# The output copies of unit 0 between the first and the second Gelu on ScalarE

## The chip, the core and the metric

One core of a Trainium2 chip (trn2) runs the whole program in one launch. The metric is the device time of one execution in microseconds. The median of three runs is 2313.62 us (2309.42 to 2320.92).

## The reference

The input x is (16, 128, 128) in float32: 16 batches of 128 tokens with 128 features. Four blocks follow one another, each added to x: a cross attention with 16 heads, a network of six layers, a second cross attention with a gate, and a network of two layers. The change lies in the six-layer network. Each of its layers is a local attention with 16 heads and then a feed-forward part:

```python
for i in range(DEPTH):                       # 6
    x = attn_layer(shift_tokens(x), Wqkv[i], q_scale[i], k_scale[i], Wo[i]) + x
    x = ffn_layer(shift_tokens(x), ln_g[i], ln_b[i], W1[i], b1[i], W2[i], b2[i]) + x
...
def ffn_layer(x, g, bln, W1, b1, W2, b2):
    ...
    hg = xn @ W1 + b1
    a, gate = jnp.split(hg, 2, -1)
    return a * jax.nn.gelu(gate, approximate=False) @ W2 + b2
```

Attention normalises q and k, rotates them, masks scores to windows of 32 tokens, takes a softmax and multiplies by v. The hidden width of the feed-forward part is 341, so a gate has 341 columns.

## The kernel before

Everything stays on chip; each engine has a queue written out by hand, in program order, and semaphores order the queues among each other. The first network runs as a software pipeline over 96 units: 6 layers times 16 batches. A unit's 16 heads are two halves of 8, which the code calls i = 0 and i = 1. In step s, `step_0(s)` of each engine handles the projections and the rotation of unit s, the transposes and (for i = 0) the scores of unit s - 1, and the rest of the attention of units s - 2 and s - 3.

For i = 0 the chain is as follows. TensorE computes the scores of unit s - 1 (`scores_all`, L751 and L757) at the end of step s. In step s + 1, which treats it as unit s - 2, ScalarE takes the Exps (`exponents_all`, L1475, first in its step), VectorE the reciprocal of the sums (L2051), GpSimd the division, TensorE the transposes (L766) and then the values (`values_all`, L780, the last work of its step). ScalarE copies the result from banks 7 and 6 of PSUM with `outputs(0, s - 2)`, two ACTIVATEs of L1506, 128x256 each. Its wait is for `AT["o"][0]`, raised by the last matmul of the values.

In the next step TensorE runs keys and queries (L700, two each at this data type: four matmuls), and then projects the values of the next unit into bank 7 (L700 as well). Bank 7 must have been copied, so that projection waits for `AT["oe"][0]`, which the second copy raises. Then follow the transposed probabilities of i = 1 (L766), a piece of the feed-forward part, a transpose of queries (L721), and the scores of i = 1, which wait for both Exp groups of i = 0 (`AG["ex"][0][0]` and `[1]`), because those read banks 3 and 4.

The feed-forward part works on groups of 4 batches, 24 groups in the first network, each spread over 4 steps; `ff_phase` gives c, the step within the group. With c == 2 the gate's three chunks (128, 128 and 85 columns) are projected (L850), VectorE copies them out (L2102), and ScalarE evaluates three Gelus in place (`ff_gelu`, L1531), each behind its own `FF["ge"]`. With c == 3 comes the up projection (L860), and VectorE multiplies it with the Gelus (L2108), chunk by chunk, each behind its `FF["gelu"]`. The step c == 2 occurs 23 times in `step_0` (s = 9, 13, ..., 97); the 24th group's Gelus are in `between`.

The end of ScalarE's step before the change:

```python
if live(s - 1):
    turned(1, s - 1, 1)
    turned(1, s - 1, 0)
if c == 2 and f >= 0:
    ff_gelu(f)
if live(s - 2):
    outputs(0, s - 2)
```

Of the kernel before, what the change touches and what calls it, by code (L numbers as in the profile page):

```python
# [8 lines left out]
ACT = mybir.ActivationFunctionType  # L9
# [14 lines left out]
CH = [(0, 128), (128, 128), (256, HID - 256)]  # L24
# [6 lines left out]
LAST = 4 * NLAYER - 1  # L31
GATE, UP = (3, 4, 5), (6, 7, 2)
# [33 lines left out]
def build(nc, A, out):  # L66
# [9 lines left out]
    with ExitStack() as ctx:  # L76
        sb = lambda name, shape, dt=F32: ctx.enter_context(nc.sbuf_tensor(name, shape, dt))
        sem = lambda name: ctx.enter_context(nc.semaphore(name))
        bank = [ctx.enter_context(nc.psum_tensor(f"bank{i}", [P, BLK], F32)) for i in range(8)]
# [15 lines left out]
        b1 = [sb(f"b1_{i}", [P, 6]) for i in range(2)]  # L95
# [49 lines left out]
        gl = [slot(39 + c) for c in range(3)]  # L145
# [29 lines left out]
        FF = {n: sem("ff_" + n) for n in "x mean cen sq var rstd bc xn aff up ge gelu hid y z outer".split()}  # L175
# [26 lines left out]
        def nth(i, p):  # L202

            return p + 1 if i == 0 else p + 1 - PHASES[1]["lo"]
# [9 lines left out]
        def at(eng, sem_, n):  # L214

            if n > 0:
                eng.wait_ge(sem_, n)

        def ff_phase(ph, s):

            t = s - ph["lo"]
            first, steps, groups = (7, 4, 24) if ph["net"] == 0 else (5, 2, 8)
            if t < first:
                return -1, -1, -1
            g, c = divmod(t - first, steps)
            f = 4 * ph["layer0"] + g
            return c, f if g < groups else -1, f - 1 if 1 <= g <= groups else -1
# [1120 lines left out]
        def _(act):  # L1348
# [89 lines left out]
            def act_phase(ph):  # L1438
# [28 lines left out]
                def exponents_all(i, p):  # L1467

                    at(act, AG["pt"][i][0], p - 1)
                    at(act, AG["ri"][i][0], p - 1)  # L1470
                    for g in range(2):
                        act.wait_ge(AG["mx"][i][g], p + 1)
                        for j in range(4):
                            h = 2 * j + g
                            ins = nc.scalar.activation(pb[i][0][p % 2][:, h * DH:(h + 1) * DH], bank[3 + g][:, j * DH:(j + 1) * DH],  # L1475
                                                       ACT.Exp, bias=amx[p % 2][:, i, h:h + 1], accum_out=asum[p % 2][:, i, h:h + 1])
                        ins.then_inc(AG["ex"][i][g], 1)
# [19 lines left out]
                def outputs(i, p):  # L1497

                    act.wait_ge(AT["o"][i], p + 1)
                    if ni == 0:  # L1500
                        at(act, AT["y"][0], p)
                    else:
                        at(act, AT["y"][i], nth(i, p - 1))
                    if ni == 0:
                        for half in range(2):
                            ins = nc.scalar.activation(o_t[i][:, 256 * half:256 * half + 256], bank[7 - half][:, 0:256], ACT.Copy)  # L1506
                        ins.then_inc(AT["oe"][i], 1)
                    else:
                        nc.scalar.activation(o_t[i], bank[7][:], ACT.Copy).then_inc(AT["oe"][i], 1)
# [11 lines left out]
                    nc.scalar.activation(fxn, fxn, ACT.Identity, scale=lnp[w][:, 0:1], bias=lnp[w][:, 1:2]  # L1521
                                         ).then_inc(FF["aff"], 1)

                def ff_gelu(f):
                    for c in range(3):
                        w = CH[c][1]
                        if f < LAST:
                            act.wait_ge(FF["ge"], 3 * f + c + 1)
                        else:
                            act.wait_ge(FF["up"], 6 * f + c + 1)  # L1530
                        nc.scalar.activation(gl[c][0:w, :], gl[c][0:w, :] if f < LAST else bank[GATE[c]][0:w, :], ACT.Gelu, bias=b1[f // 4 % 2][0:w, 3 + c:4 + c]  # L1531
                                             ).then_inc(FF["gelu"], 1)

                def step_0(s):
                    c, f, before = ff_phase(ph, s)
                    if live(s - 2):
                        exponents_all(0, s - 2)
                        values(0, s - 2)
                    if live(s - 3):
                        probs_all(1, s - 3)  # L1540
                    if live(s):
                        square(0, s, 1)
                        square(0, s, 0)
                    if s == 0:
                        gate_weights()
                    if live(s - 1):
                        turned(0, s - 1, 0)
                    if live(s - 3):
                        outputs(1, s - 3)
                    if s in (1, 3, 5):  # L1550
                        g_square(act, (s + 1) // 2, (s + 1) // 2)
                    if c == 0 and f >= 0:
                        ff_square(f)
                    if c == 1 and f >= 0:
                        ff_affine(f)
                    if live(s - 2):
                        exponents_all(1, s - 2)
                    if live(s):
                        square(1, s, 1)
                        square(1, s, 0)  # L1560
                    if live(s - 1):
                        turned(0, s - 1, 1)
                    if s == hi:
                        for k in range(2):
                            g_square(act, 4 + k, k)
                    if live(s - 2):
                        probs_all(0, s - 2)
                        values(1, s - 2)
                    if live(s - 1):
                        turned(1, s - 1, 1)  # L1570
                        turned(1, s - 1, 0)
                    if c == 2 and f >= 0:
                        ff_gelu(f)
                    if live(s - 2):
                        outputs(0, s - 2)

                def step_1(s):
                    c, f, before = ff_phase(ph, s)
                    if live(s - 3):
                        outputs(1, s - 3)  # L1580
                    if live(s - 2):
                        exponents(1, s - 2, 0)
                        probs(0, s - 2, 0)
                        exponents(1, s - 2, 1)
                    if live(s):
                        square(0, s, 0)
                    if live(s - 1):
                        turned(0, s - 1, 0)
                        turned(0, s - 1, 1)
                    if s - lo in (1, 3):  # L1590
                        n = 10 + (s - lo - 1) // 2
                        g_square(act, n, n - 8)
                    if c == 0 and f >= 0:
                        ff_square(f)
                    if live(s):
                        square(0, s, 1)
                    if live(s - 2):
                        values(0, s - 2)
                        probs(0, s - 2, 1)
                    if c == 1 and f >= 0:  # L1600
                        ff_gelu(f)
                    if live(s - 1):
                        exponents(0, s - 1, 1)
                        exponents(0, s - 1, 0)
                    if live(s - 2):
                        probs(1, s - 2, 1)
                        probs(1, s - 2, 0)
                    if live(s):
                        square(1, s, 0)
                    if c == 0 and f >= 0:  # L1610
                        ff_affine(f)
                    if live(s - 2):
                        values(1, s - 2)
                    if live(s - 1):
                        turned(1, s - 1, 1)
                    if live(s):
                        square(1, s, 1)
# [4 lines that stand above are left out]
# [48 lines left out]

            t0, ff0_square, ff0_affine, ff0_gelu = act_phase(PHASES[0])
            t1, _a, _b, _c = act_phase(PHASES[1])

            def between(s, part):

                if (s, part) == (1, 1):
                    ff0_square(23)
                if (s, part) == (2, 1):
                    ff0_affine(23)
                    g_square(act, 6, 2)  # L1680
                if (s, part) == (3, 2):
                    ff0_gelu(23)
                if (s, part) == (5, 1):
                    g_square(act, 7, 3)
                if s in (7, 9) and part == 0:
                    n = 8 + (s - 7) // 2
                    g_square(act, n, n - 8)
# [764 lines left out]
```

## Time and profile before

| | us |
|---|---|
| median of 3 runs | 2313.62 |
| lowest and highest run | 2309.42, 2320.92 |
| the profiled execution | 2317.28 |
| its span, first to last instruction | 2315.5 |

| engine | busy, share of the span |
|---|---|
| TensorE, matmuls (PE) | 2135.8 us, 92% |
| TensorE, weight loads (PEld, beside PE) | 1456.9 us, 63% |
| VectorE (DVE) | 1759.7 us, 76% |
| ScalarE (ACT) | 1708.7 us, 74% |
| GpSimd (POOL) | 1339.4 us, 58% |

One execution was recorded. A row of a timeline gives the start in us from the start of the span, the duration, the engine, the line of the program, the operation, the tiles written and read, and in brackets the idle time of the engine before it with what ended it. "issue" means that the engine waited for nothing that the profile shows. Matmul rows of one line that follow each other are merged (xN), and so are activations; instructions of one engine overlap a little, so N of them take less than N durations. Shares of busy time are averages over stages with different limits, so the waits and one place in order of time say more than the table.

### The profile page before, as it was taken

Reading aid. Unit: us, or ns where it says so; the run is one execution under the profiler, and the core shown is the slowest. Engines: PE = TensorE matmul, PEld = TensorE weight load, DVE = VectorE, ACT = ScalarE, POOL = GpSimd, SP = SyncE. Lnnn points to the kernel's source line nnn. Section 1 sums busy time; section 2 is a strip of 40 time slices with the busy share of each in tenths; the row PEclk is TensorE's granted clock in tenths of the full one; section 3 lists DMA queues with packets and bytes.
Section 4 is the critical chain, followed back from the end, with each engine's and each line's share of the span. In section 5 each row is a group of like instructions: output and inputs, shape, how many; then the busy total and the mean of one; then the engine's idle time right before and its main releaser. Section 6 shows DMA issues by size and latency. Waiting matters only on the chain. (4 is left out here: it accounts for less than half of the span.)

```text
span 2315.5 us, 88378 instructions
## 1 busy us (share of the span) xinstructions
PE 2135.8 (92%) x33770; PEld 1456.9 (63%) x33770; DVE 1759.7 (76%) x4937; ACT 1708.7 (74%) x5910; POOL 1339.4 (58%) x1270
## 2 busy tenths in 40 slices
PE   7989999999999989999999999999999886899997
PEld 5656666666666666666666666666666664666663
DVE  4888777778777878777777777877777477887863
ACT  3757787877788877787787787877787544788783
POOL 1347666666666666666666666766666124666650
PEclk8999999999999999999999999999999998999999
DMA  4001221112211222112211122111221100000000
GB/s 111 4 3 40 67 57 46 39 47 66 56 41 40 64 50 55 40 43 62 55 48 43 44 66 58 47 38 43 53 52 41 44 13 7 13 13 15 15 11 23
DMA packets 144687, 96.93 MB, mean 42 GB/s; under 512 B 61928, under 2 KB 137232, under 8 KB 144272
## 3 DMA queue, kind: packets, MB, share of 16 engines
q1 hardware_dynamic: 143120, 91.02, 15.5%
q8 instruction: 274, 4.49, 0.8%
q14 instruction: 141, 1.16, 0.2%
q10 hardware_dynamic: 1152, 0.26, 0.1%
HBM read 23.11 MB, written 1.05 MB: 10 GB/s over the span
## 5 line engine op out<-in xcount | busy, mean ns | idle before, releaser
L700 PE MATMUL bank<-wqkv,hs 128*128 128x512 f32 x1344 | 675.1, 621 | 19.0 <-ACT arena L1506 13.5
L1779 POOL TENSOR_TENSOR arena<-arena,rnorm 128x512 f32<-128x512 f32 x448 | 455.2, 1044 | 388.7 <-DVE rnorm L2028 387.5
L1772 POOL TENSOR_TENSOR arena<-arena 128x512 f32<-128x512 f32 x448 | 567.0, 1273 | 140.4 <-DVE arena L1977 140.4
L1475 ACT ACTIVATE arena<-bank,amx 128x64 f32<-128x64 f32 x1536 | 457.5, 334 | 8.3 <-DVE amx L2043 8.0
L1972 DVE TENSOR_TENSOR arena<-bank,rot 128x512 f32<-128x512 f32 x448 | 306.7, 685 | 88.9 <-PE bank L700 85.3
L700 PEld LDWEIGHTS bank<-wqkv,hs 128*128 128x128 f32 x1344 | 230.9, 193 | 207.1 <-issue 158.1
L1452 ACT ACTIVATE arena<-bank 128x512 f32<-128x512 f32 x448 | 263.9, 616 | 131.3 <-PE bank L721 130.1
L1475 ACT ACTIVATION_READ_ACCUMULATOR arena<-bank,amx 128x1 f32 x1536 | 351.1, 229 | 0.0
L1977 DVE TENSOR_TENSOR arena<-bank,rot 128x256 f32<-128x256 f32 x896 | 333.4, 413 | 0.0
L721 PEld LDWEIGHTS bank<-ident,arena 128*128 128x128 f32 x1792 | 212.9, 142 | 151.7 <-issue 128.5
L1984 DVE TENSOR_REDUCE ss<-arena 128x8 f32<-128x512 f32 x448 | 283.3, 669 | 31.2 <-ACT arena L1446 31.0
L1446 ACT ACTIVATE arena<-bank 128x512 f32<-128x512 f32 x448 | 265.0, 644 | 44.5 <-DVE arena L1977 44.0
L1786 POOL TENSOR_TENSOR arena<-arena,ainv 128x512 f32<-128x512 f32 x192 | 200.3, 1043 | 165.4 <-DVE ainv L2051 165.4
L721 PE MATMUL bank<-ident,arena 128*128 128x128 f32 x1792 | 251.7, 275 | 12.5 <-POOL arena L1779 5.8
L1506 ACT ACTIVATE arena<-bank 128x256 f32<-128x256 f32 x384 | 127.1, 387 | 178.7 <-PE bank L780 177.8
L813 PEld LDWEIGHTS bank<-arena,wo 128*128 128x128 f32 x1792 | 220.9, 194 | 56.5 <-issue 50.0
L780 PE MATMUL bank<-arena 64*64 64x32 f32 (+1 forms) x9216 | 186.3, 221 | 51.3 <-issue 50.0
L813 PE MATMUL bank<-arena,wo 128*128 128x128 f32 x1792 | 225.7, 278 | 3.1 <-ACT arena L1506 2.6
L780 PEld LDWEIGHTS bank<-arena 64*64 64x64 f32 x9216 | 160.7, 134 | 73.2 <-issue 56.5
L2043 DVE TENSOR_REDUCE amx<-bank 128x4 f32<-128x256 f32 x384 | 143.8, 416 | 39.7 <-PE bank L757 39.4
L757 PE MATMUL bank<-arena 64*32 64x64 f32 (+1 forms) x12288 | 168.7, 217 | 0.0
L757 PEld LDWEIGHTS bank<-arena 64*32 64x32 f32 x12288 | 154.8, 105 | 0.3
(179 smaller groups left out, 3224.5 us busy)
## 6 DMA issues: line engine op xcount, KB each, us to landing
arena<-arena SPq DMA_DIRECT2D x768, 64.0 KB
wqkv<-in_L_ffn_Wqkv_dram SPq DMA_DIRECT2D x24, 256.0 KB, 3.1
hs<-z SPq DMA_DIRECT2D x128, 32.0 KB, 1.8
fx<-z SPq DMA_DIRECT2D x32, 128.0 KB, 2.2
hs<-z SPq DMA_DIRECT2D x128, 31.8 KB, 1.9
fx<-z SPq DMA_DIRECT2D x32, 127.0 KB, 2.5
wqkv<-in_L_ffn_Wqkv_dram SPq DMA_DIRECT2D x24, 128.0 KB, 2.5
w<-in_L_ffn_W_dram SPq DMA_DIRECT2D x6, 341.0 KB
```

Source lines behind the costliest of these rows:

```text
L700: nc.tensor.matmul(bank[o][:], src[:], wqkv[w][:, off:off + 512], start=True, stop=True).then_inc(AT[name] if part < 2 else AT[name][i], 1)
L721: mm = nc.tensor.transpose(bank4[o][:, j, :], rc[i][c][p % 2][:, j * P:(j + 1) * P], ident[:])
L757: mm = nc.tensor.matmul(bank[3 + g][q:q + 32, DH * j:DH * j + n], q_t[i][rows, P * j + q:P * j + q + 32], k_t[i][rows, P * j + key:P * j + ...
L780: mm = nc.tensor.matmul(bank4[7 - half][to:to + DH, j, q0:q1], src[g][rows, DH * h:DH * h + DH], pbt[i][0][rows, h * P + q0:h * P + q1], s ...
L813: mm = nc.tensor.matmul(bank4[7][:, 0, :], wo[w][:, i, j, :] if ni == 0 else wo[w][:, j // 2, j % 2, :], o_t[i][:, j * P:(j + 1) * P], sta ...
L1446: nc.scalar.activation(sq[i][c], bank[c][:], ACT.Square).then_inc(AT["sqk" if c else "sqq"], 1)
L1475: ins = nc.scalar.activation(pb[i][0][p % 2][:, h * DH:(h + 1) * DH], bank[3 + g][:, j * DH:(j + 1) * DH], ACT.Exp, bias=amx[p % 2][:, i, ...
L1772: nc.gpsimd.tensor_tensor(t, t, rs[i][c], ALU.add).then_inc(AT["ak" if c else "aq"][i], 1)
L1779: nc.gpsimd.tensor_tensor(t, t, rnorm[p % 2][:, i, HU * c:HU * c + HU].unsqueeze(2).to_broadcast([P, HU, DH]), ALU.mult).then_inc(AT["mk" ...
L1972: nc.vector.tensor_tensor(heads(rc[i][c][p % 2]), src, r[:, 2 * c, :].unsqueeze(1).to_broadcast([P, HU, DH]), ALU.mult)
L1977: ins = nc.vector.tensor_tensor(dst, src[:, :, (1 - a) * hd:(2 - a) * hd], r[:, 2 * c + 1, a * hd:(a + 1) * hd].unsqueeze(1).to_broadcast( ...
L1984: nc.vector.tensor_reduce(ss[:, i, HU * c:HU * c + HU], heads(sq[i][c]), AX.X, ALU.add).then_inc(AT["ssk" if c else "ssq"], 1)
```

## The change

On ScalarE, `ff_gelu(f)` ran a loop over three chunks; `ff_gelu(f, c)` now runs one chunk. In `step_0`, `outputs(0, s - 2)` stood behind the three Gelus and now stands behind the first. In `step_1` (second network) and in `between` (the 24th group) the three calls are made in a loop, in the order of before. No other engine's program is changed.

```diff
--- before.py
+++ after.py
@@ -1521,15 +1521,15 @@
                     nc.scalar.activation(fxn, fxn, ACT.Identity, scale=lnp[w][:, 0:1], bias=lnp[w][:, 1:2]
                                          ).then_inc(FF["aff"], 1)
 
-                def ff_gelu(f):
-                    for c in range(3):
-                        w = CH[c][1]
-                        if f < LAST:
-                            act.wait_ge(FF["ge"], 3 * f + c + 1)
-                        else:
-                            act.wait_ge(FF["up"], 6 * f + c + 1)
-                        nc.scalar.activation(gl[c][0:w, :], gl[c][0:w, :] if f < LAST else bank[GATE[c]][0:w, :], ACT.Gelu, bias=b1[f // 4 % 2][0:w, 3 + c:4 + c]
-                                             ).then_inc(FF["gelu"], 1)
+                def ff_gelu(f, c):
+
+                    w = CH[c][1]
+                    if f < LAST:
+                        act.wait_ge(FF["ge"], 3 * f + c + 1)
+                    else:
+                        act.wait_ge(FF["up"], 6 * f + c + 1)
+                    nc.scalar.activation(gl[c][0:w, :], gl[c][0:w, :] if f < LAST else bank[GATE[c]][0:w, :], ACT.Gelu, bias=b1[f // 4 % 2][0:w, 3 + c:4 + c]
+                                         ).then_inc(FF["gelu"], 1)
 
                 def step_0(s):
                     c, f, before = ff_phase(ph, s)
@@ -1570,9 +1570,12 @@
                         turned(1, s - 1, 1)
                         turned(1, s - 1, 0)
                     if c == 2 and f >= 0:
-                        ff_gelu(f)
+                        ff_gelu(f, 0)
                     if live(s - 2):
                         outputs(0, s - 2)
+                    if c == 2 and f >= 0:
+                        ff_gelu(f, 1)
+                        ff_gelu(f, 2)
 
                 def step_1(s):
                     c, f, before = ff_phase(ph, s)
@@ -1598,7 +1601,8 @@
                         values(0, s - 2)
                         probs(0, s - 2, 1)
                     if c == 1 and f >= 0:
-                        ff_gelu(f)
+                        for chunk in range(3):
+                            ff_gelu(f, chunk)
                     if live(s - 1):
                         exponents(0, s - 1, 1)
                         exponents(0, s - 1, 0)
@@ -1679,7 +1683,8 @@
                     ff0_affine(23)
                     g_square(act, 6, 2)
                 if (s, part) == (3, 2):
-                    ff0_gelu(23)
+                    for c in range(3):
+                        ff0_gelu(23, c)
                 if (s, part) == (5, 1):
                     g_square(act, 7, 3)
                 if s in (7, 9) and part == 0:
```

## Rows read from the trace of the kernel before

**Rows 1.** The page: the span; busy time, share of it and instructions by engine.
```profile
span 2315.5 us, 88378 instructions
...
PE 2135.8 (92%) x33770; PEld 1456.9 (63%) x33770; DVE 1759.7 (76%) x4937; ACT 1708.7 (74%) x5910; POOL 1339.4 (58%) x1270
```

**Rows 2.** Groups of ScalarE: line, operation, shape, count | busy us, mean ns | idle before.
```profile
L1531 ACT ACTIVATE arena<-arena,b 128x512 f32<-128x512 f32 x62 | 41.3, 714 | 0.4
L1531 ACT ACT_TABLE_LOAD x31 | 39.8, 1283 | 0.5
...
L1475 ACT ACT_TABLE_LOAD x22 | 28.2, 1283 | 0.4
```

**Rows 3.** Waits of TensorE in the whole run: total us, times, longest.
```profile
PE bank L780 <- issue: 50.0, 66, 3.4
...
PE bank L700 <- ACT arena L1506: 13.5, 16, 0.9
```

**Rows 4.** ScalarE in time, one place: start, us, line, operation, [idle before].
```profile
506.45 0.66 ACT L1506 ACTIVATE arena<-bank 128x256 f32<-128x256 f32 x2 [1.75 <-PE bank L780]
...
513.23 1.08 ACT L1452 ACTIVATE arena<-bank 128x512 f32<-128x512 f32 x2
514.33 1.28 ACT L1531 ACT_TABLE_LOAD   x1
515.63 1.95 ACT L1531 ACTIVATE arena<-arena,b 128x512 f32<-128x512 f32 x3
517.48 0.63 ACT L1506 ACTIVATE arena<-bank 128x256 f32<-128x256 f32 x2
518.13 1.28 ACT L1475 ACT_TABLE_LOAD   x1
519.42 0.31 ACT L1475 ACTIVATE arena<-bank,amx 128x64 f32<-128x64 f32 x1
...
521.65 0.24 ACT L1475 ACTIVATION_READ_ACCUMULATOR arena<-bank,amx 128x1 f32 x1
```

**Rows 5.** TensorE in time, the same place.
```profile
505.99 0.42 PE L780 MATMUL bank<-arena 64*64 64x32 f32 x11 [0.71 <-issue]
...
514.49 0.90 PE L780 MATMUL bank<-arena 64*64 64x64 f32 x48
515.32 1.99 PE L700 MATMUL bank<-wqkv,hs 128*128 128x512 f32 x4
518.16 1.13 PE L700 MATMUL bank<-wqkv,hs 128*128 128x512 f32 x2 [0.85 <-ACT arena L1506]
...
521.99 0.30 PE L751 MATMUL bank<-mask_b,ident_b 64*32 64x256 bf16 x8 [0.97 <-issue]
```

**Rows 6.** VectorE in time, the same place.
```profile
521.98 0.20 DVE L2051 RECIPROCAL ainv<-asum 128x8 f32<-128x8 f32 x1 [2.39 <-issue]
522.10 0.74 DVE L2108 SCALAR_TENSOR_TENSOR arena<-bank,b,arena 128x512 f32<-128x512 f32 x1
...
528.62 0.75 DVE L2108 SCALAR_TENSOR_TENSOR arena<-bank,b,arena 128x512 f32<-128x512 f32 x1 [0.57 <-PE bank L860]
```

**Rows 7.** First, largest and last late place: the Gelus, then TensorE's values.
```profile
305.87 1.95 ACT L1531 ACTIVATE arena<-arena,b 128x512 f32<-128x512 f32 x3
...
306.27 0.67 PE L780 MATMUL bank<-arena 64*64 64x32 f32 x32 [1.16 <-issue]
...
1061.28 1.95 ACT L1531 ACTIVATE arena<-arena,b 128x512 f32<-128x512 f32 x3
...
1062.16 0.42 PE L780 MATMUL bank<-arena 64*64 64x32 f32 x11 [1.25 <-issue]
...
1753.45 1.95 ACT L1531 ACTIVATE arena<-arena,b 128x512 f32<-128x512 f32 x3
...
1753.96 0.66 PE L780 MATMUL bank<-arena 64*64 64x32 f32 x28 [1.11 <-issue]
```

## The prediction

> **What bounds the kernel now.** I read the page first. TensorE is busy 92% of the span and ScalarE 74% [rows 1], so a gain has to come out of TensorE's idle time, or out of a stretch where ScalarE sets the pace. The change touches 23 places, one step in four of the first network's 96 units: the step in which ScalarE evaluates the three Gelus of a feed-forward group. So the next view is what ScalarE spends on Gelus [rows 2], then the waits of the whole run [rows 3], then one such place in order of time on ScalarE [rows 4], TensorE [rows 5] and VectorE [rows 6], and last the places that look different [rows 7].
>
> TensorE waited 13.5 us in all, 16 times, for the output copies of L1506 before a projection of L700 [rows 3]. By the trace 15 of these waits lie right behind the Gelus, 0.82 to 0.87 us each; this is the wait that the edit can remove. In the place near 514 us, ScalarE turns queries (L1452), loads the Gelu table from 514.33, runs three Gelus from 515.63, makes the two output copies from 517.48, loads the Exp table from 518.13, and runs 8 Exps from 519.42; their last record ends at 521.65 + 0.24 = 521.89 [rows 4]. The reader is to see that no row from 513.23 to there has idle time before it: ScalarE runs 8.7 us without a pause. TensorE meanwhile ends its values at 514.49 + 0.90 = 515.39, ends the next step's four key and query matmuls at 517.31, waits 0.85 us for the copies until 518.16, and then waits again, 0.97 us, before the scores at 521.99 [rows 5]. That second wait ends 0.10 us behind the Exps; `scores_all` waits there for both groups of them, since they read the score banks that it overwrites. The profile calls it "issue", but the program's wait and the time agree. VectorE also stands still, 2.39 us, and resumes at 521.98 with the reciprocals of the Exps' sums [rows 6]. So here ScalarE's queue, from the Gelu table to the last Exp, is the path, and TensorE has 0.85 + 0.97 us of slack in it.
>
> **The change part by part.** It adds and removes no instruction and no wait. On ScalarE the two copies go ahead of the second and third Gelu, in the 23 steps with c == 2; the rewritten calls in `step_1` and `between` give the old order. TensorE's, VectorE's, GpSimd's and SyncE's queues are the same, and ScalarE issues no DMA here.
>
> The copies come earlier. A Gelu starts about (1.95 - 0.71) / 2 = 0.62 us behind the one before [rows 2, 4], so the copies can start 1.24 us sooner, at 516.25, and end at 516.9. TensorE is busy until 517.31, so its wait of 0.85 us goes. What is late next is the second wait: projection, transposes and the up projection all move 0.85 us forward, and then TensorE stands 0.97 + 0.85 = 1.82 us before the scores, for the last Exp is where it was. VectorE is held by the same Exps. Gain: 0.00 us per place. The rest of ScalarE's queue up to the last Exp holds the same work in another order, so its length is the same but for how neighbours overlap: the load would follow a Gelu (0.71 us long, 0.62 us apart) and no longer a copy. I take zero; the overlap of two neighbours is about 0.1 us by these rows, so the bounds are -0.1 and +0.1 us per place, -2.3 and +2.3 us in 23.
>
> The second and third Gelu come 0.65 us later. Their readers are the products with the up projection on VectorE (L2108). The first of these starts at 522.10 and needs only the first Gelu, which doesn't move; the second starts at 528.62, the third behind it [rows 6]. Cost nothing; were this cover gone, at most 0.65 us per place.
>
> The copies wait for TensorE's values (L780), and now the Gelus and Exps are queued behind that wait. In 15 places the values end about 0.86 us before the second Gelu's old start (515.39 against 516.25 [rows 4, 5]) and the wait is open. In 7 places TensorE stands for 0.83 to 1.25 us in the middle of the values, a stall that the profile calls "issue", and the values end later: at 306.27 + 0.67 = 306.94 in the first, where the second Gelu began at 305.87 + 0.62 = 306.49, so 0.44 us too late (unrounded starts); 0.67 us in the largest (1062.58 against 1061.90) and 0.54 in the last [rows 7]. The four others, read the same way, give 0.57, 0.28, 0.52 and 0.32. Sum 3.34 us. A waiting copy starts 0.04 us behind the values' end (506.45 against 505.99 + 0.42 [rows 4, 5]): 7 * 0.04 = 0.28. Before the change a Gelu filled this time; now ScalarE idles, and the Exps, TensorE's scores and VectorE's reciprocals come later by as much. In these places TensorE doesn't wait for the copies now, so nothing is given back. The cost may be less where a later stall of TensorE swallows it; such a stall, of 1.4 us or more, stands 2 to 3 us behind the Exps in two of the seven (the sizes 0.67 and 0.32), so the bounds are 2.5 and 3.6 us. I take 3.6, since TensorE's queue has no spare time between most of these scores and the next step. The 23rd place closes the phase, its values are ready in time and no scores stand behind it; I cost it at zero.
>
> Sum: 0 + 3.6 = +3.6 us. Against the profiled execution, 2317.28 us with a span of 2315.5 us, this is 2320.9. That execution is 3.7 us over the median of the runs, 2313.62 us; on the median the sum gives 2317.2 us.
>
> **The rivals.**
> A. TensorE's wait is worth its length. If the stretch were TensorE's and not ScalarE's, each of the 15 waits would come off the time: 13.5 * 15 / 16 = 12.7 us, less the 3.6 us that rival A would also deny (TensorE would have slack for them). Time 2300.9. For it speaks that TensorE is the busiest engine; against it the 0.97 us wait right behind, which ends with the Exps. It decides if the scores don't wait for Exps there. A half-way case, in which some of the 0.85 us survives because stalls of TensorE shift, gives about 2307.
> B. Slower: the stall inside the values meets more places. Stalls before L780 sum to 50.0 us in 66 waits [rows 3], and only 7 of 23 places have one now. It costs from the point where the values end behind the second Gelu's start, 0.86 us later than in an open place; the smallest stall among the seven, 0.83 us, already ends them 0.28 + 0.86 = 1.14 us later, so this point lies at a stall of some 0.55 us. If all 23 places had it, at the mean of the seven, (3.34 + 0.28) / 7 = 0.52 us, the cost would be 11.9 us, time 2325.5. Against it: TensorE's own stream is unchanged, and the work ahead of these values too.
> C. Slower: the copy between two Gelus forces the tables to change. A load is 1.28 us [rows 2]; two more per place, 23 * 2 * 1.28 = 59 us, time 2373. Against it: the copies already follow the third Gelu with no load between (517.48), and the load stands only before the first Exp [rows 4].
> The Trainium skill, in "ScalarE: Activation LUTs", section "Table sets: the hidden batching unit", tells authors to group activations by table set and finish one before switching, which speaks against putting another function between two Gelus; but it also lists copy among the cheap functions present in every set, and the trace agrees, with 0 loads between Gelu and copy. By the same page's section on the load, a switch costs about 2.66 us with its drain, which would make C some 122 us; the trace has 0.02 us between the turned keys' end and the load.
> D. The change doesn't do what it says. If the built queue kept the old order, the time would stay at 2313.6 us; against it, the queue in the trace follows the program's order call by call [rows 4].
>
> **How the numbers follow.** Forecast (0 to +6 us, nothing gained behind the copies) 0.80; A 0.07; half-way 0.03; B 0.06; C 0.02; D 0.02. Predicted: 2317.2. The likeliest case's own bounds are 2.5 - 2.3 = +0.2 and 3.6 + 2.3 = +5.9 us, and runs of one kernel here differ by 4 to 7 us from their median. The range goes from 2304 to 2325: it leaves out A, C and part of B, and takes in the half-way case. A measurement of this kernel can tell about 0.5%, 11.6 us, from no change. Faster by more: A and a little of the half-way case, 0.08. Slower by more: B and C, 0.08. Within: 0.84.
>
> **What would show it.** Right: on ScalarE one Gelu, two copies, two Gelus, one load, 8 Exps; the wait of L700 for L1506 falls from 13.5 us to about 1; the wait before L751 behind it grows from 0.97 to about 1.8 us; in about 7 places the copies show idle time of 0.3 to 0.7 us with L780 as releaser, and the Exps' end stays 7.56 us behind the Gelu table's load in the other places. Wrong: a wait before L751 that doesn't grow (A), copies that wait in many more than 7 places (B), or more than 31 loads at L1531 (C). The weakest step is that the stalls inside TensorE's blocks stay where they are.

## The result and the profile after

The kernel with the change takes 2326.78 us (median of 9 runs, 2314.49 to 2330.3) against 2311.05 us of the kernel before (9 runs in the same session). The ratio is 1.0057, with a 95% interval of 1.0040 to 1.0073: 0.4% to 0.7% slower, about 13 us. A second measurement (e4, below) gives 1.0070, 1.0049 to 1.0091. The forecast was +3.6 us, 2317.2 us on the median, with a range of 2304 to 2325 us. The median of 2326.78 us lies 1.8 us above that range; 1.0057 times the 2311.05 us of the kernel before is 2324.2 us, just inside it.

The page of the profiled execution (2327.74 us): span, busy time, and the group of projections (line, operation, shape, count | busy us, mean ns | idle time before, longest releaser).

```profile
span 2326.0 us, 88378 instructions
...
PE 2140.6 (92%) x33770; PEld 1463.3 (63%) x33770; DVE 1761.2 (76%) x4937; ACT 1711.2 (74%) x5910; POOL 1339.7 (58%) x1270
...
L700 PE MATMUL bank<-wqkv,hs 128*128 128x512 f32 x1344 | 676.0, 624 | 6.2 <-ACT arena L1446 2.5
```

The same number of instructions, and of TensorE's 13.5 us of waiting for the copies in 16 waits [rows 3] one wait is left. The waits of TensorE in the run after say where they went (total us, times, longest):

```profile
PE bank L780 <- issue: 46.0, 62, 2.8
PE bank L751 <- issue: 40.4, 22, 2.1
...
PE bank L700 <- ACT arena L1506: 0.8, 1, 0.8
```

The stalls inside the values are of the size of before (50.0 us). The wait ahead of the scores, L751, is 40.4 us in 22 waits; in the kernel before it was this:

```profile
PE bank L751 <- issue: 19.8, 22, 1.0
```

One open place in order of time, first ScalarE, then TensorE; it answers to [rows 4, 5].

```profile
513.06 1.28 ACT L1531 ACT_TABLE_LOAD   x1
514.35 0.72 ACT L1531 ACTIVATE arena<-arena,b 128x512 f32<-128x512 f32 x1
514.98 0.64 ACT L1506 ACTIVATE arena<-bank 128x256 f32<-128x256 f32 x2
515.51 1.33 ACT L1531 ACTIVATE arena<-arena,b 128x512 f32<-128x512 f32 x2
...
520.38 0.23 ACT L1475 ACTIVATION_READ_ACCUMULATOR arena<-bank,amx 128x1 f32 x1
```

```profile
514.05 2.84 PE L700 MATMUL bank<-wqkv,hs 128*128 128x512 f32 x6
516.73 0.60 PE L766 MATMUL bank<-ident,arena 128*128 128x128 f32 x4
517.16 1.02 PE L860 MATMUL bank<-arena,w 128*128 128x512 f32 x2
518.02 0.60 PE L721 MATMUL bank<-ident,arena 128*128 128x128 f32 x4
520.72 0.30 PE L751 MATMUL bank<-mask_b,ident_b 64*32 64x256 bf16 x8 [2.09 <-issue]
```

From the table's load to the last Exp it is 520.61 - 513.06 = 7.55 us, as before (7.56). TensorE runs keys, queries and the projection without a pause, six matmuls in one row, and then stands for 2.09 us in one piece where it stood 0.85 and 0.97 us.

A late place: the first Gelu, the copies and the other Gelus; then TensorE's values and scores.

```profile
789.74 0.72 ACT L1531 ACTIVATE arena<-arena,b 128x512 f32<-128x512 f32 x1
791.23 0.66 ACT L1506 ACTIVATE arena<-bank 128x256 f32<-128x256 f32 x2 [0.77 <-PE bank L780]
791.77 1.32 ACT L1531 ACTIVATE arena<-arena,b 128x512 f32<-128x512 f32 x2
```

```profile
790.51 0.66 PE L780 MATMUL bank<-arena 64*64 64x32 f32 x30 [1.38 <-issue]
...
796.98 0.30 PE L751 MATMUL bank<-mask_b,ident_b 64*32 64x256 bf16 x8 [1.30 <-issue]
```

The copies wait 0.77 us for the values. All 7 late places do so, by 0.07 to 0.77 us, with 3.28 us in sum, and their Exps end 4.02 us later in sum, counted from the table's load.

These 4 us aren't 13. The rest stands in the granted clock. The windows view, 6 us from the start of the scores (columns: stretch, length, busy us of each engine with its instructions, granted share of TensorE's clock, DMA share, GB/s), first of before, then of after:

```profile
core 0: us, PE busy (x) PEld busy (x) DVE busy (x) ACT busy (x) POOL busy (x), PEclk, DMA share, GB/s
380.99:386.99 6.00, 3.90 (x123) 2.54 (x124) 3.25 (x7) 4.12 (x16) 2.73 (x3) 0.90 0.22 55
452.77:458.77 6.00, 5.83 (x142) 4.46 (x143) 5.46 (x13) 5.76 (x25) 4.04 (x4) 1.00 0.22 57
521.99:527.99 6.00, 5.83 (x141) 4.46 (x142) 5.46 (x13) 5.76 (x25) 4.00 (x4) 1.00 0.22 53
```

```profile
450.25:456.25 6.00, 5.83 (x131) 4.12 (x132) 4.14 (x10) 5.35 (x23) 2.73 (x3) 0.72 0.23 57
520.72:526.72 6.00, 5.83 (x142) 4.46 (x143) 5.46 (x13) 5.76 (x25) 4.00 (x4) 1.00 0.22 55
657.90:663.90 6.00, 5.85 (x130) 3.86 (x131) 4.46 (x10) 5.75 (x24) 2.97 (x4) 0.72 0.23 59
727.34:733.34 6.00, 6.00 (x134) 4.51 (x134) 4.44 (x10) 5.62 (x24) 2.92 (x4) 0.72 0.23 57
1003.07:1009.07 6.00, 5.83 (x130) 4.12 (x131) 4.12 (x10) 5.46 (x23) 2.70 (x3) 0.72 0.24 60
```

Of the 15 open places with scores, 14 of before have a granted clock of 1.00, and one has 0.90. (In three of the 15, near 381, 862 and 1346 us, a stall of 1.92, 1.60 and 1.36 us inside the values follows the scores; the 0.90 stands behind the first of them.) After, 6 of the 15 have 0.72: in a part of the stretch the clock is at 1.2 GHz instead of 2.4. It fell 0.5 to 1.7 us behind the scores' start, when TensorE was at work again. TensorE's busy time in such a stretch is the same and it finishes less: 131 matmuls against 142. The same values and projection as rows:

```profile
451.38 1.51 PE L780 MATMUL bank<-arena 64*64 64x64 f32 x48 [0.17 <-issue]
452.81 2.90 PE L700 MATMUL bank<-wqkv,hs 128*128 128x512 f32 x4
```

They take 1.51 and 2.90 us, where an undisturbed place takes 0.90 and 1.99 [rows 5], 1.5 us more together. The table-to-table distance of the groups in these six places is 8.25 us longer in sum than in the kernel before, 1.4 us each. Over the whole run the mean granted clock fell from 0.981 to 0.977. Half speed in a stretch loses the share that the clock lacks, so 0.019 * 2315.5 = 44.0 us of before become 0.023 * 2326.0 = 53.5 us: 9.5 us more, and the clocks are rounded, so give or take 2 us. With the 4.0 us of later Exps this makes 13.5 us, the size of the measured loss of 13 to 16 us. The two profiled executions themselves differ by 10.5 us (2327.74 against 2317.28), so for this pair the sum is some 3 us too large. One pair can't say how much of the clock's part belongs to the change; the experiments have to. The nine runs say the same: the fastest (2314.49 us) had a mean clock of 0.982, the one with 2328.64 us had 0.976.

### The profile page after: what moved, and what is told of

Its sections match the earlier page's. It is cut to its first block and busy times, and to the rows that moved or that the text cites. A ratio compares the mean times of both kernels' runs of the same rounds, so it can differ in the third digit from the quotient of the medians.

```text
span 2326.0 us, 88378 instructions
## 1 busy us (share of the span) xinstructions
PE 2140.6 (92%) x33770; PEld 1463.3 (63%) x33770; DVE 1761.2 (76%) x4937; ACT 1711.2 (74%) x5910; POOL 1339.7 (58%) x1270
## 5 line engine op out<-in xcount | busy, mean ns | idle before, releaser
L1452 ACT ACTIVATE arena<-bank 128x512 f32<-128x512 f32 x448 | 263.8, 616 | 134.8 <-PE bank L721 133.5
```

## The experiments

The theory after this reading has two causes: ScalarE's idle time ahead of waiting copies (4 us), and a joined idle time of TensorE behind which the clock falls more often (some 10 us). One rival puts all on ScalarE's queue and calls the clock chance; the other puts all on the clock. "Low stretch" in the expectations is one stretch of 3.4 us at half clock in the trace. Between 300 and 1830 us the kernel before has 5 of them and the change 12. Every kernel was measured beside the kernel before on one chip; ratios are to that.

### e1 and e2: the change in one kind of place only

```diff
+                    early = f not in (0, 4, 7, 11, 14, 18, 21)    # e1; e2: f in (...)
                     if c == 2 and f >= 0:
-                        ff_gelu(f, 0)
+                        for chunk in range(1 if early else 3):
+                            ff_gelu(f, chunk)
                     if live(s - 2):
                         outputs(0, s - 2)
-                    if c == 2 and f >= 0:
+                    if c == 2 and f >= 0 and early:
                         ff_gelu(f, 1)
                         ff_gelu(f, 2)
```

> The copies move ahead of the second and third Gelu only in the 16 places where TensorE's values are ready in time; in the 7 late places (groups 0, 4, 7, 11, 14, 18, 21) the order is the old one. Theory (two causes: ScalarE's idle time before waiting copies, about 4 us, and a fall of TensorE's granted clock to 0.5 for 3.4 us behind the joined idle time of 2.09 us before the scores, about 1.5 us each, 7 more of them): ScalarE waits nowhere for the copies in these places, the joined idle time is in the 15 open places, and the time is 7 to 12 us over the kernel before, with 4 to 9 more low stretches of the clock than before between 300 and 1830 us. Rival 1 (all of the loss is ScalarE's queue behind the waiting copies, the clock differs by chance): no change, within 2 us. Rival 2 (all is the clock): the whole loss of the change, 13 us or more.

Measured: 2324.25 us against 2313.37, ratio 1.0053 (1.0035 to 1.0072), 12 us slower. ScalarE waits for no copy in the 23 places, and the Exps end at 7.56 us in all of them. The granted clock behind the joined idle time fell again in 6 of 15 open places, and there are 12 low stretches, 7 more than before; two of the places:

```profile
444.31:450.31 6.00, 5.83 (x130) 3.84 (x131) 4.45 (x10) 5.74 (x24) 2.96 (x4) 0.72 0.23 57
1343.35:1349.35 6.00, 4.83 (x122) 3.43 (x123) 2.78 (x6) 4.07 (x16) 2.71 (x3) 0.52 0.21 54
```

This run settles most of it: no engine does more, no queue ends later in these places, and yet the kernel is slower by an amount that ScalarE's queue can't give. Rival 1 falls.

> The copies move only in the 7 late places (groups 0, 4, 7, 11, 14, 18, 21). Theory: the copies wait in these 7 places for 3 us in all, the Exps end about 4 us later in sum, no idle time of 2.09 us arises, the clock's low stretches are as many as before (about 5 between 300 and 1830 us), and the time is 3 to 5 us over the kernel before. Rival 1: the whole loss, 11 to 16 us. Rival 2: 0 to 1 us.

Measured: 2320.66 us, ratio 1.0035 (1.0021 to 1.0049), 8 us, interval 5 to 11. The copies waited for 2.99 us in the 7 places and the Exps ended 3.72 us later in sum, as expected; the clock fell within 6 us of the scores' start in 3 of the 22 places, against 2 before. Rival 2 falls, since this part alone costs. The expectation of 3 to 5 us is just missed. There are 8 low stretches where about 5 were expected; what the other 4 us are isn't shown, though 1.6 us of them go with the runs' clock (table under e11). TensorE's idle time before the scores grew in these places from 0.6 to 0.9 us to 1.3 us, but the trace shows no clear harm from it. e1 and e2 together, 20 us, are a little more than the whole, 13 to 16, within their intervals.

### e3 and e9: TensorE's idle time split again

e3 adds a wait of the projection for the third Gelu, with ScalarE's new order kept; e9 puts that wait in place of the one for the copies, so that no instruction is added. The edit of e9:

```diff
+                        c, f, before = ff_phase(ph, s - 1)
+                        if c == 2 and f >= 0:
+                            pe.wait_ge(FF["gelu"], 3 * f + 3)
-                        if live(s - 3):
+                        elif live(s - 3):
                             at(pe, AT["oe"][0], s - 2)
```

> The change as it is, and TensorE's projection behind the copies also waits for the third Gelu, so that its idle time is split again, about 0.85 us before the projection and 1.0 us before the scores. Theory: ScalarE's waits stay (about 4 us), the joined idle time of 2.09 us and the extra low stretches of the clock go, so the time is 3 to 6 us over the kernel before, that is, about 10 us below the change. Rival 1: the split does nothing, 13 to 16 us over before. Rival 2: as fast as before.

Measured: 2317.12 us, ratio 1.0018 (1.0003 to 1.0033), 4 us slower than before, so about 10 us faster than the change, by an added wait. The numbers fit, but not cleanly: the 23 added waits moved the stalls inside the values, which fell to 42.0 us and met ScalarE's copies in 4 places instead of 7. Hence e9.

> The change, and TensorE's projection behind the copies waits for the third Gelu in place of the copies (which ScalarE makes earlier). No instruction is added on any engine, so the stalls inside TensorE's blocks keep their places, which the run with an added wait could not ensure. Idle time is split again: about 0.85 us before the projection, 0.9 to 1.0 us before the scores. Theory of two causes: ScalarE's waits for the copies stay (3 to 4 us), the joined idle time goes, 3 to 7 us over the kernel before. Rival (the loss comes with the order on ScalarE, however TensorE's idle time is cut): 12 to 16 us over before.

Measured: 2321.57 us, ratio 1.0023 (1.0005 to 1.0040), 5 us. The copies waited in the same 7 places, and the Exps ended 5 us later in sum. There are 7 low stretches. TensorE in one open place:

```profile
516.92 1.13 PE L700 MATMUL bank<-wqkv,hs 128*128 128x512 f32 x2 [0.86 <-ACT arena L1534]
520.75 0.30 PE L751 MATMUL bank<-mask_b,ident_b 64*32 64x256 bf16 x8 [0.98 <-issue]
```

The six microseconds behind it, in the windows view:

```profile
520.75:526.75 6.00, 5.82 (x141) 4.46 (x142) 5.46 (x13) 5.76 (x25) 3.99 (x4) 1.00 0.23 57
```

The clock fell in 2 of 22 places, as before the change. With ScalarE's order and waits left as the change has them, cutting TensorE's 2.09 us into 0.86 and 0.98 takes away about two thirds of the loss (the intervals of e9 and the first measurement of the change touch at 1.0040; e4's lies clear of e9's). What is left, 5 us, is what the Exps are late.

### e4: the change once more

> The change itself, beside the three others on the same chip. Both theories: 10 to 16 us over the kernel before; by the theory of two causes with 10 to 12 low stretches of the clock between 300 and 1830 us, most of the extra ones starting right behind the scores that follow the idle time of 2.09 us.

Measured: 2327.94 us, ratio 1.0070 (1.0049 to 1.0091), 15 us. The clock fell behind the joined idle time in 6 of 15 open places, four of them the same as in the first profile and two others: it isn't tied to a place. There are 10 low stretches, as expected.

### e5, e6 and e8: work in the idle time

```diff
-                    for j in range(4):
+                    for j in list(range(4)) * rounds:
                         mm = nc.tensor.transpose(bank4[o][:, j, :], rc[i][c][p % 2][:, j * P:(j + 1) * P], ident[:])
...
-                        turn(0, s - 1, 0, "mq", "qt")
+                        c, f, before = ff_phase(ph, s)
+                        turn(0, s - 1, 0, "mq", "qt", 4 if c == 3 and f >= 0 else 1)    # e6, e8: 2
```

> The change, and in the step behind the Gelus TensorE makes the four transposes of queries that stand ahead of the scores three times more (12 extra transposes, the same data into the same bank), some 1.3 us of work in the joined idle time of 2.09 us. ScalarE's queue is that of the change. Theory of two causes: the idle time before the scores falls to about 0.8 us, the extra low stretches of the clock go, ScalarE's waits (3 to 4 us) stay, and the time is 3 to 6 us over the kernel before although work was added. Rival (the joined idle time has no part in it): 13 to 16 us over before, as the change.

> As the one with 12, with one more round of the transposes (4 extra, some 0.45 us): idle time about 1.65 us before the scores. Theory: between the change and the one with 12 extra, 5 to 14 us over before, and not above the change. Rival: 13 to 16 us over before.

> The kernel before with 4 extra transposes in the same place: its idle time before the scores falls from 0.97 to about 0.5 us. Theory: few of the clock's low stretches of before come from these 0.97 us, so the time stays within 3 us; it is the control for the added instructions themselves. If short idle times count as well, up to 5 us faster; if the extra transposes cost time by themselves, up to 10 us slower.

Measured: the change with 12 extra transposes 2322.54 us, ratio 1.0035 (1.0018 to 1.0052), 9 us over before; with 4 extra 2334.43 us, ratio 1.0087 (1.0064 to 1.0109), 21 us; the kernel before with 4 extra 2324.04 us, ratio 1.0041 (1.0023 to 1.0059), 11 us. The control says why the first two miss their numbers: extra instructions cost some 11 us by themselves, though they lie in idle time. Against that control, the change costs 10 us with 1.65 us of idle time left. And the step from 4 to 12 extra transposes, more work on the busiest engine, makes the kernel 12 us faster. The rows of e5 show the idle time that is left:

```profile
509.32 1.91 PE L721 MATMUL bank<-ident,arena 128*128 128x128 f32 x16
512.01 0.30 PE L751 MATMUL bank<-mask_b,ident_b 64*32 64x256 bf16 x8 [0.78 <-issue]
```

Behind 0.9 us or less (e5) the clock fell in 2 of 22 places, behind 1.65 us (e6) in 5 of 15. Why the extra transposes cost 11 us in the control isn't settled: they shift where TensorE's stalls lie (3.8 us more of them before projections there), which is part of it at most.

### e7: the copies between the second and the third Gelu

> The copies stand between the second and the third Gelu. They start 0.62 us later than in the change, about where the late values end: ScalarE waits for 0.1 to 0.4 us in all; TensorE waits 0.2 us before the projection and about 1.9 us before the scores. Theory of two causes: ScalarE's 4 us go, most of the clock's part stays, 5 to 11 us over before. If ScalarE's waits were all of it: no change against before. If the copies' place as such cost time: as the change, 13 to 16 us.

Measured: 2319.85 us, ratio 1.0021 (1.0004 to 1.0039), 5 to 7 us. ScalarE waited 0.96 us for the copies, TensorE 0.25 us before the projection and 1.58 us before the scores; the Exps were 1.3 us late in sum. The clock fell in 8 of 15 open places, one of them here:

```profile
524.61:530.61 6.00, 5.83 (x130) 3.84 (x131) 4.45 (x10) 5.74 (x24) 2.94 (x4) 0.72 0.22 54
```

So the clock fell behind 1.58 us in one piece as well. The profiled execution, 2331.31 us, was the slowest of its 12 runs, and its count is high for this kernel.

All profiles together: behind an idle time of 1.5 us or more the clock fell within 6 us in 31 of 75 places (change 6 of 15, e4 6 of 15, e1 6 of 15, e7 8 of 15, e6 5 of 15). In the profiles with 1.0 us or less in every place it fell in 2 of 22 (before, e3, e5, e9, e10, e11) or 3 of 22 (e8).

### e10: one Gelu instead of three

If ScalarE's stretch from the Gelu table to the last Exp is the path in these places, then shortening it must pay in full. The bias moves to VectorE's copy out of PSUM, and one Gelu of 1536 columns over the three chunks' tiles (`gl_all`) replaces three. It has to wait for all three chunks at once.

```diff
-                    nc.vector.tensor_copy(gl[c][0:w, :], bank[2][0:w, :]).then_inc(FF["ge"], 1)
+                    nc.vector.tensor_scalar(gl[c][0:w, :], bank[2][0:w, :], b1[f // 4 % 2][0:w, 3 + c:4 + c], None, ALU.add
+                                            ).then_inc(FF["ge"], 1)
...
+                    if f < LAST:
+                        act.wait_ge(FF["ge"], 3 * f + 3)
+                        at(act, FF["hid"], 3 * f)
+                        nc.scalar.activation(gl_all, gl_all, ACT.Gelu).then_inc(FF["gelu"], 3)
+                        return
```

> The kernel before, with the gate's bias added by VectorE as it copies each chunk out of PSUM, and one Gelu over 1536 columns where three of 512 stood, in front of the output copies (the last group of the second network keeps its three). The Gelus take about 1.95 us now; one of 1536 columns about 1.6 us by the rows (0.71 us for 512 columns and twice 512 columns at the rate between 0.38 us for 256 and 0.62 us for 512), so ScalarE's stretch from the table to the last Exp is 0.3 to 0.4 us shorter. Theory (that stretch is the path in these places): TensorE's waits before the projection and the scores shorten, and the time falls by 23 places at 0.3 to 0.4 us, 7 to 9 us below the kernel before, and some more if low stretches of the clock go with them. Rival (TensorE's queue is the path there): within 2 us of before.

Measured: 2305.88 us against 2315.72, ratio 0.9961 (0.9948 to 0.9975), 9 us faster than the kernel before. ScalarE in one place:

```profile
504.83 1.28 ACT L1529 ACT_TABLE_LOAD   x1
506.13 1.48 ACT L1529 ACTIVATE arena<-arena 128x1536 f32<-128x1536 f32 x1
507.52 0.64 ACT L1507 ACTIVATE arena<-bank 128x256 f32<-128x256 f32 x2
...
511.71 0.24 ACT L1476 ACTIVATION_READ_ACCUMULATOR arena<-bank,amx 128x1 f32 x1
```

The one Gelu takes 1.48 us instead of 1.95, and the stretch is 511.95 - 504.83 = 7.12 us instead of 7.56, 0.44 us less. 23 * 0.44 = 10.1 us against 9 us measured. TensorE's waits for the copies fall from 13.5 to 7.0 us:

```profile
PE bank L701 <- ACT arena L1507: 7.0, 16, 0.8
```

The rival, that TensorE's queue is the path there, would have given nothing. This is the fastest version of the study.

### e11: the kernel before, one more profile

> The kernel before once more, for one more profile of it: time and mean granted clock as a pair. Theory: 2305 to 2323 us, ScalarE's stretch from the Gelu table to the last Exp 7.56 us in all places, 5 to 8 low stretches of the clock, and a time that follows the mean granted clock at about 2.3 us for each 0.001 of it.

Measured: 2310.32 us at a mean granted clock of 0.986, against 2317.28 us at 0.981. All places have 7.56 us, and the clock fell behind the scores in 2 of 22. Here 0.001 of clock was worth 1.4 us; over the nine runs of the change it is 2.0 us by a straight line. Both are below the 2.3 us expected; that TensorE is idle in part of a low stretch would explain it, but wasn't measured.

All runs on record for which the clock was noted, 177 of them, can be put together. Within a kernel, time falls by 2.0 us for each 0.001 of mean granted clock. So each kernel's distance to the kernel before, measured beside it, splits into a part that goes with the clock and a rest. The rest can be held against how late the Exps are in that kernel's profile (us; the rest is good to about 2 us):

| | mean time over before | with the clock | rest | Exps late, in sum |
|---|---|---|---|---|
| e4, the change | 14.2 | 9.8 | 4.4 | 4.3 |
| e1, open places | 11.0 | 11.2 | -0.2 | 0.0 |
| e2, late places | 6.8 | 1.6 | 5.3 | 3.7 |
| e9, idle time split | 5.6 | 1.3 | 4.3 | 4.8 |
| e3, split by an added wait | 4.3 | 3.5 | 0.7 | 2.6 |
| e7, copies second | 6.9 | 5.1 | 1.8 | 1.3 |
| e5, 12 transposes | 8.4 | 3.5 | 5.0 | 4.0 |
| e6, 4 transposes | 21.6 | 13.2 | 8.3 | 4.8 |
| e8, before with 4 | 10.2 | 4.8 | 5.4 | 0.0 |

This is the cleanest reading of the two causes. In e1 the loss goes with the clock and nothing is left. In e2 and e9 little goes with the clock, and the rest is of the size of the late Exps. The change has both. Only e6 and e8, with their added transposes, keep 3 to 5 us that neither cause explains.

## Why the prediction was right or wrong

**TensorE's wait for the copies is worth nothing: right.** It fell from 13.5 to 0.8 us, as said, and the wait before the scores took it over, because the Exps hadn't moved. The mechanism that was named, ScalarE as the path from 514.33 to 521.89, holds in after (7.55 us) and e10 confirms it from the other side. The size was off a little: 2.09 us instead of 1.82, since keys, queries and projection take 2.84 us in one row, where they took 1.99 + 1.13 us with the pause between. Rival A falls.

**ScalarE's waits in the 7 late places, +3.6 us: right in place and in sum, place by place partly luck.** It is the same 7 places, and their Exps end 4.0 us later. The sizes, counted as in the prediction from the second Gelu's old start to the end of the values, came out as 0.71, 0.31, 0.81, 0.12, 0.52, 0.60 and 0.54 us, where the trace of before had 0.44, 0.57, 0.28, 0.67, 0.52, 0.32 and 0.54. The sum, 3.6 us, is near the 3.34 worked out, but only two of seven places kept their size: the step that the prediction called its weakest, stalls that stay where they are, holds for the places and not for the lengths. A copy started 0.04 us behind the values, as taken. (The profile's idle time of ScalarE, 3.28 us, is smaller than the delay, since it begins with the end of the first Gelu, and an undelayed copy overlaps that Gelu by 0.09 us: 514.98 against 514.35 + 0.72.) Rival B falls: no further place was late. e2 and e9 put this part at 5 to 8 us, with intervals that reach down to 1 us (e9) and 5 us (e2).

**The order of neighbours on ScalarE, zero: right.** 7.55 against 7.56 us. Rival C falls too, with no added load of a table. (The load that the prediction puts 0.02 us behind the turned keys stands behind the turned queries, the second of the two ACTIVATEs of L1452.)

**"Gain: 0.00 us per place": the step that failed.** The prediction added 0.85 and 0.97 us of idle time to one piece and let it cost nothing, because nobody waits for TensorE there. It never asked what the piece does to TensorE's clock. The missing term is 15 open places, of which 6 had a fall at about 1.5 us: 9 us. That is why the time is some 13 to 16 us above before and not 3.6. The range reaches the neighbourhood of the measured time only through the room that had been kept for rival B, which is another mechanism; that is luck. With its own bounds, +0.2 to +5.9 us, the likeliest case missed. The chances were wrong as well: with this term, slower by about 0.5% was the likeliest outcome, where 0.08 was given to it.

What would have shown it in the trace of before: between 300 and 1830 us TensorE has 8 stalls of 1.5 us or more, all inside the values. Behind 4 of them the clock was low within the next 6 us of work; behind its 47 idle times of 0.8 to 1.2 us, only 2 times. Two of the stalls, and the windows behind four of the eight:

```profile
865.47 0.31 PE L780 MATMUL bank<-arena 64*64 64x32 f32 x6 [1.60 <-issue]
1071.14 0.55 PE L780 MATMUL bank<-arena 64*64 64x64 f32 x24 [1.82 <-issue]
```

```profile
384.84:390.84 6.00, 6.00 (x29) 3.97 (x30) 2.99 (x7) 4.10 (x20) 1.27 (x1) 0.72 0.14 35
865.47:871.47 6.00, 6.00 (x37) 4.25 (x38) 3.99 (x10) 4.76 (x22) 1.42 (x2) 1.00 0.22 55
1071.14:1077.14 6.00, 6.00 (x45) 3.87 (x45) 2.73 (x7) 4.14 (x20) 1.27 (x1) 0.72 0.14 36
1590.42:1596.42 6.00, 6.00 (x37) 4.00 (x37) 2.90 (x7) 4.79 (x21) 3.43 (x3) 0.72 0.10 26
```

The edit makes a wait of the first kind out of two of the second, in 15 places. By these rows an estimate is 15 * 4 / 8 falls at 1.5 us each, some 11 us beside the 3.6. In all thirteen profiles the clock fell behind 66 of 115 such stalls outside the scores, somewhat more often than behind the joined idle time.

## What to carry to other kernels

When a reordering only moves a wait, look at how the idle time is cut, too: two short waits of TensorE can be cheaper than one of the same sum. A wait that the profile shows on the busiest engine is worth removing only if the next wait behind it isn't for the same engine; here both were ScalarE's, and what paid was to make ScalarE's own stretch shorter. Put a copy that waits for another engine behind work that is ready, unless the engine that needs it can use the time.

## What the runs showed of the hardware

TensorE's granted clock fell in a kernel in which TensorE is busy 92% of the time. Behind idle times of 1.6 to 2.2 us before the scores it was at 1.2 GHz for a part of the next 6 us in 31 of 75 places, each at 1.4 to 1.5 us of lost time; behind 1.0 us or less, in 2 or 3 of 22 places of a profile. Between 300 and 1830 us stalls of 1.5 us or more inside TensorE's other blocks, nearly all in the values, were followed by such a fall in 66 of 115 cases. It isn't tied to a place: runs of one kernel differ in it, and that is much of their spread of 16 us.

Instructions put into idle time weren't free: 4 extra transposes in each of 23 places, some 0.45 us in a wait of 0.97 us, cost 11 us (e8); about half of it goes with the clock, the rest is unexplained.
